# Second feed-forward stage: rows normalised on ScalarE as scale and bias, the residual sum in two halves

## The chip, the cores and the metric

The kernel runs on one core of a Trainium2 chip. A core has TensorE (PE, with its weight loads shown apart as PEld), VectorE (DVE), ScalarE (ACT), GpSimd (POOL) and a queue for transfers (SP), each with its own stream of instructions; they meet at semaphores. The metric is the device time of one execution in microseconds (us); the median of the runs is compared.

## The reference

One transformer block on x of shape 2 x 4096 x 256, in float32:

```python
x = x + 0.5 * ffn(layernorm(x), Wr, We)          # first feed-forward stage
x = x + attention(layernorm(x), ...)             # 16 heads of 16
x = x + 0.5 * ffn(layernorm(x), Wr, We)          # second feed-forward stage

def layernorm(x, eps=1e-05):
    m = mean(x); v = var(x)                      # over the 256 of a row
    return (x - m) / sqrt(v + eps)

def ffn(x, Wr, We):                              # E = 8 experts, TOP_K = 2
    logits = einsum('btd,ed->bte', x, Wr)
    top_vals, top_idx = top_k(logits, 2)
    w = softmax(top_vals)
    # a token is dropped by an expert that is full (C = T*2/8*1.5 + 1)
    return einsum('btk,btkd->btd', w, expert_outputs)
```

## The kernel before

The program has three phases one after the other: the first feed-forward stage with the projections for q, k and v (names beginning with fr_), attention (at_), and the second feed-forward stage with attention's output projection in front of it (bk_). The change is in the third, `back_phase`.

The 8192 rows are worked in 16 groups of 512 rows, each as TG = 4 tiles of 128 rows by 256. The text counts bodies 0 to 15: in body g the experts of group g are computed and, between them, the groups g+1 and g+2 are prepared. Bodies 0 and 1 and the last four stand written out in the program, the ten between are a loop of two bodies a pass. The order on every engine is the order in which the code is written; there is no planner.

The experts. All eight experts are applied to all rows and weighted afterwards, most weights being zero. A body has 16 chunks, numbered 0 to 15 here: four tiles (i) by four pairs of experts (k). A chunk is six matmuls of 128x512 into one of three PSUM banks (`pe_s`, `NB = 3`, `experts`, L1417). VectorE then takes the chunk up with two operations, one for each expert (`combine`, L1547): out = bank * weight + what was summed so far. A bank is used again every third chunk (only the last chunk takes bank 1 early), so TensorE waits at chunk n for VectorE's second operation on chunk n-3.

The preparation of a later group, in the order of its data:

- `spread_out` (PE, L1368) spreads the softmax reciprocals into bank `py[0]`; `normalise_heads` (DVE, L1495) multiplies attention's output by them into `an`; `project` (PE, L1374) multiplies `an` by Wo into both banks `py[0]` and `py[1]`.
- `biased` (POOL, L1637) adds the output bias to the residual x into `xb`; `add_residual` (DVE, L1502) adds `py` and `xb` into `y[u]`, two operations of 128x512.
- `statistics` (DVE, L1510 to L1517) finds mean and variance of the four tiles (`mv`, `var`); `take_root` (ACT, L1459) takes the root; the Newton steps in `normal` (DVE, L1523 to L1527) make one over the root (`rs`), each waiting for the one before.
- the last four operations of `normal` (DVE, L1531) write xn = (y - mean) * rs, one of 128x256 for each tile.
- `turn` (PE, L1384) transposes `xn` into `pT`; `turned` (ACT, L1466 and L1468) copies that to `xt` and `xh`; `lower` (POOL, L1642) makes the low part `xl`; `router` (PE, L1393) makes the logits; `pick` (DVE, L1562 to L1572), `route` (POOL), `exponential` (ACT, L1474), `odds` (DVE), `positions` (PE), `room` (DVE, L1579) and `weigh` (POOL, L1674) make the weights.

In body g, VectorE's turn is: chunks 0 and 1, statistics(g+1), chunks 2 and 3, normal(g+1), chunks 4 and 5, normalise_heads(g+2), chunks 6 to 9, pick(g+1), chunks 10 to 13, odds(g+1), chunks 14 and 15, room(g+1), add_residual(g+2). In body 0 the inversion of the softmax sums of the second batch (`invert_sums`, L1217 to L1221) stands behind pick. TensorE's turn is: chunks 0 to 3, spread_out(g+2), chunks 4 to 7, turn(g+1), chunks 8 and 9, router(g+1), project(g+2), chunks 10 to 15, positions(g+1). ScalarE's is: take_root, turned, exponential.

The first feed-forward stage (`front_phase`) already has the form that the change brings to the third phase: `newton` ends with `nb` = -mean * rs (DVE, L580), and `normalise` (ACT, L476) writes xn.

Of the kernel before, what the change touches and what calls it, by code (L numbers as in the profile page):

```python
# [21 lines left out]
ALU = mybir.AluOpType  # L22
# [3 lines left out]
P = 128  # L26
# [7 lines left out]
TG = 4  # L34
# [7 lines left out]
def hold(eng, sem, value, tick):  # L42

    eng.wait_ge(sem, value)
    eng.sem_inc(tick, 1)
# [31 lines left out]
def need(eng, sem, value):  # L77

    if not (isinstance(value, int) and value <= 0):
        eng.wait_ge(sem, value)  # L80
# [1167 lines left out]
def back_phase(nc, name, shared, ahead, sources, attended_out, out):  # L1248
# [7 lines left out]
    BANK = [n % NB for n in range(CHUNKS - 1)] + [1]  # L1256
    PICKS = 11
    ROUTE = 7
    with ExitStack() as ctx:
        def sb(n, shape, dt=F32):  # L1260
            return ctx.enter_context(nc.sbuf_tensor(f"{name}_{n}", shape, dt))
# [14 lines left out]
        xn, xt = sb("xn", [P, TG, D]), sb("xt", [P, NC, GT])  # L1276
        xh, xl = ([sb(f"{n}{u}", [P, NC, GT], F32R) for u in range(2)] for n in ("xh", "xl"))
        stats, mv = sb("stats", [P, TG, 6]), sb("mv", [P, TG, 2])
        var, root, r0, r1, rs = (sb(n, [P, TG]) for n in ("var", "root", "r0", "r1", "rs"))
        acc, acb = [sb(f"acc{u}", [P, TG, D]) for u in range(2)], sb("acb", [P, 2, D])  # L1280

        t1, t2, left, a0, a1, mask = (sb(n, [P, TG, E]) for n in ("t1", "t2", "left", "a0", "a1", "mask"))
# [32 lines left out]
        def runs(g, ahead):  # L1315

            return not isinstance(g, int) or g + ahead < NG

        with nc.Block() as block:
# [43 lines left out]
            def _(pe):  # L1363
                def spread_out(n, u, it):

                    pe.wait_ge(s_rec[u], it * DMA + DMA)
                    need(pe, s_y, n)
                    pe.matmul(py[0][:, :], spread[:, :], rec[u][:, :], start=True, stop=True).then_inc(s_pr, 1)  # L1368

                def project(n):  # L1370
                    need(pe, s_an, n + 1)
                    for i in range(TG):
                        for c in range(NC):
                            last = pe.matmul(py[i // 2][:, (i % 2) * D:(i % 2 + 1) * D], an[:, c, i * P:(i + 1) * P],  # L1374
                                             wo[:, c, :], start=(c == 0), stop=(c == NC - 1))
                    last.then_inc(s_py, 1)
# [78 lines left out]
            @block.scalar  # L1455
            def _(ac):
                def take_root(n):
                    need(ac, s_var, n + 1)
                    ac.activation(root[:, :], var[:, :], ACT.Sqrt).then_inc(s_root, 1)  # L1459

                def turned(n, u):

                    need(ac, s_tr, n + 1)
                    need(ac, s_xl, n)
                    for c in range(NC):
                        ac.activation(xt[:, c, :], pT[c][:, :], ACT.Copy)  # L1466
                    for c in range(NC):
                        last = ac.activation(xh[u][:, c, :], pT[c][:, :], ACT.Copy)  # L1468
                    last.then_inc(s_ev, 1)

                def exponential(n):
                    need(ac, s_gap, n + 1)
                    need(ac, s_wt, n)
                    ac.activation(ex[:, :], gap[:, :], ACT.Exp).then_inc(s_ex, 1)  # L1474

                take_root(0)
                turned(0, 0)
                exponential(0)

                def body(g, u, it):  # L1480
                    if runs(g, 1):
                        take_root(g + 1)
                        turned(g + 1, 1 - u)
                        exponential(g + 1)

                iterations(ac, body)

            @block.vector
            def _(ve):
# [5 lines left out]
                        last = ve.tensor_tensor(an[:, c, :], at[u][:, c, :], py[0][:, :], ALU.mult)  # L1495
                    last.then_inc(s_an, 1)

                def add_residual(n, u):
                    ve.wait_ge(s_py, n + 1)
                    ve.wait_ge(s_xb, n + 1)  # L1500
                    for k in range(2):
                        last = ve.tensor_tensor(y[u][:, 2 * k:2 * k + 2, :].rearrange("p i d -> p (i d)"), py[k][:, :],  # L1502
                                                xb[:, 2 * k:2 * k + 2, :].rearrange("p i d -> p (i d)"), ALU.add)
                    last.then_inc(s_y, 1)

                def statistics(n, src):

                    hold(ve, s_y, n + 1, s_tick)
                    for i in range(TG):
                        last = ve.bn_stats(stats[:, i, :], src[:, i, :])  # L1510
                    last.then_inc(s_a, 1)
                    hold(ve, s_a, n * 2 + 1, s_tick)
                    for i in range(TG):
                        last = ve.bn_aggr(mv[:, i, :], stats[:, i, :])  # L1514
                    last.then_inc(s_a, 1)
                    ve.wait_ge(s_a, n * 2 + 2)
                    ve.tensor_scalar(var[:, :], mv[:, :, 1], EPS, None, ALU.add).then_inc(s_var, 1)  # L1517

                def normal(n, src):

                    ve.wait_ge(s_root, n + 1)
                    ch = Chain(ve, s_nw, 5, n)
                    ch.step(ve.reciprocal(r0[:, :], root[:, :]))  # L1523
                    ch.step(ve.tensor_tensor(r1[:, :], r0[:, :], r0[:, :], ALU.mult))  # L1524
                    ch.step(ve.tensor_tensor(rs[:, :], r1[:, :], var[:, :], ALU.mult))  # L1525
                    ch.step(ve.tensor_scalar(r1[:, :], rs[:, :], -0.5, 1.5, ALU.mult, ALU.add))  # L1526
                    ch.step(ve.tensor_tensor(rs[:, :], r0[:, :], r1[:, :], ALU.mult))  # L1527
                    ch.close()
                    need(ve, s_tr, n)
                    for i in range(TG):  # L1530
                        last = ve.tensor_scalar(xn[:, i, :], src[:, i, :], mv[:, i, 0:1], rs[:, i:i + 1],  # L1531
                                                ALU.subtract, ALU.mult)
                    last.then_inc(s_xn, 1)

                def combine(g, u, it, i, first=0, end=E):
                    if i == 0 and first == 0:
# [53 lines left out]
                ve.wait_ge(s_bv, 1)  # L1590
                ve.tensor_tensor(bo_sb[:, :], bo_sb[:, :], py[1][:, 0:D], ALU.add).then_inc(s_bo, 1)
                normalise_heads(0, 0, 0)
                add_residual(0, 0)
                statistics(0, y[0])
                normal(0, y[0])
                normalise_heads(1, 1, 0)
                pick(0)
                odds(0)
                room(0)
                add_residual(1, 1)  # L1600

                def body(g, u, it):
                    combine(g, u, it, 0, 0, E // 2)
# [1 line left out]
                        statistics(g + 1, y[1 - u])  # L1605
                    combine(g, u, it, 0, E // 2, E)
                    if runs(g, 1):
                        normal(g + 1, y[1 - u])
                    combine(g, u, it, 1, 0, E // 2)
                    if runs(g, 2):  # L1610
                        normalise_heads(g + 2, u, it + 1)
# [1 line left out]
                    combine(g, u, it, 2, 0, E // 2)  # L1613
                    if runs(g, 1):
                        pick(g + 1)
                    if isinstance(g, int) and g == 0:
                        invert_sums(ve, ahead, 1)
                    combine(g, u, it, 2, E // 2, E)
# [4 lines left out]
                    if runs(g, 1):  # L1623
                        room(g + 1)
                    if runs(g, 2):
                        add_residual(g + 2, u)

                iterations(ve, body)

# [1 line left out]
            def _(gp):  # L1631
                def biased(n, u, it):
                    hold(gp, s_x[u], it * DMA + DMA, s_tick)
                    if not (isinstance(n, int) and n == 0):
                        hold(gp, s_y, n, s_tick)
                    for i in range(TG):
                        last = gp.tensor_tensor(xb[:, i, :], xg[u][:, i, :], bo_sb[:, :], ALU.add)  # L1637
                    last.then_inc(s_xb, 1)
# [150 lines left out]
```

## Time and profile before

| | us |
|---|---|
| median of 3 runs | 6290.88 |
| lowest and highest | 6289.6, 6301.9 |
| the profiled execution | 6298.43 |
| its span | 6296.6 |
| its third phase, from about 5779 to the end | 517 |

| engine | busy us | share of the span |
|---|---|---|
| PE | 6199.1 | 98% |
| DVE | 5929.1 | 94% |
| ACT | 4830.8 | 77% |
| POOL | 398.3 | 6% |

Most of the span is attention, which the change leaves alone. The shares of the whole span therefore tell little of the third phase; its own stretches are read instead. Stretches of the trace are given in us from the start of the span. A row of the timeline has the start, the time, the engine, the line, the operation, what it writes and reads, and how many were merged into the row; in brackets stands the engine's idle time before it and what ended that. A "<-" after an engine in a list of waits names whom it waited for.

### The profile page before, as it was taken

What the parts mean: (1) busy time and instruction counts of PE and PEld (TensorE: products, weight loads), DVE (VectorE), ACT (ScalarE), POOL (GpSimd) and SP (SyncE); (2) the same over time, 40 slices, a digit from 0 to 9 for tenths busy, and PEclk for the clock granted to TensorE, in tenths of its full rate; (3) what the DMA queues carried; (4) which work ended last, traced back from release to release, by engine and by line L of the source; (5) the groups of instructions that cost most, each with busy time, mean ns of one, the idle gap of its engine ahead of it and who ended that gap; (6) DMA issues with size and microseconds to landing.
All of it is one profiled execution on the core that took longest, in us unless ns stands there. A gap on an engine that the chain in (4) does not pass through costs nothing. (4 is left out here: it accounts for less than half of the span.)

```text
span 6296.6 us, 158218 instructions
## 1 busy us (share of the span) xinstructions
PE 6199.1 (98%) x54276; PEld 2765.3 (44%) x54276; DVE 5929.1 (94%) x6835; ACT 4830.8 (77%) x8889; POOL 398.3 (6%) x604
## 2 busy tenths in 40 slices
PE   8998999999999999999999999999999999999999
PEld 6886333333333333333333333333333333334777
DVE  7998999999999999999999999999999999992877
ACT  4443488888888888888888888888888888886111
POOL 3443100000000000000000000000000000000221
PEclk9998699999999999999999999999999999999999
DMA  2334110101010101010101010101010101000110
GB/s 85 121 126 124 25 17 14 17 14 17 13 17 14 17 14 17 14 17 14 17 14 17 14 17 14 17 14 17 14 17 14 17 14 17 3 22 26 60 52 28
DMA packets 121411, 175.90 MB, mean 28 GB/s; under 512 B 62016, under 2 KB 78944, under 8 KB 117728
## 3 DMA queue, kind: packets, MB, share of 16 engines
q1 hardware_dynamic: 120928, 168.25, 11.8%
q8 instruction: 451, 7.39, 0.5%
q14 instruction: 32, 0.26, 0.0%
HBM read 98.47 MB, written 69.73 MB: 27 GB/s over the span
## 5 line engine op out<-in xcount | busy, mean ns | idle before, releaser
L1136 DVE TENSOR_REDUCE at_mx<-at_m 128x1 f32<-128x1024 f32 x4027 | 4927.9, 1224 | 47.6 <-PE at_m L1012 28.1
L1111 ACT ACTIVATE at_ex<-at_s 128x512 f32<-128x512 f32 x8192 | 4450.2, 595 | 612.9 <-PE at_s L1033 44.7
L1033 PE MATMUL at_s<-at_q,at_k 50*128 50x512 f32 x8192 | 2998.4, 444 | 0.0
L1012 PE MATMUL at_m<-at_k,at_q 48*128 48x512 f32 x8032 | 2927.1, 444 | 0.0
L1043 PE MATMUL at_po<-at_ex,at_v 128*32 128x256 f32 x32816 | 2625.8, 392 | 0.0
L1012 PEld LDWEIGHTS at_m<-at_k,at_q 48*128 48x128 f32 x8032 | 1184.3, 185 | 1658.7 <-DVE at_mx L1136 1590.5
L1043 PEld LDWEIGHTS at_po<-at_ex,at_v 128*32 128x32 f32 x32816 | 646.6, 108 | 1489.4 <-issue 749.9
L1033 PEld LDWEIGHTS at_s<-at_q,at_k 50*128 50x128 f32 x8192 | 1212.4, 185 | 42.6 <-ACT at_ex L1111 42.2
L987 POOL COPY at_v<-at_vst 128x1024 f32<-128x1024 f32 x16 | 16.7, 1041 | 4463.6 <-DMA at_vst<-v_by_head 4463.4
L1417 PE MATMUL bk_ps<-sh_weh,bk_xl 128*128 128x512 f32 x512 | 170.1, 413 | 20.2 <-DVE bk_acc L1547 20.1
L1459 ACT ACTIVATE bk_root<-bk_var 128x4 f32<-128x4 f32 x16 | 3.3, 205 | 218.0 <-DVE bk_var L1517 218.0
L1417 PE MATMUL bk_ps<-sh_weh,bk_xh 128*128 128x512 f32 x512 | 160.8, 395 | 0.0
L1417 PE MATMUL bk_ps<-sh_wel,bk_xh 128*128 128x512 f32 x512 | 160.8, 395 | 0.0
L1547 DVE SCALAR_TENSOR_TENSOR bk_acb<-bk_ps,bk_weight,bk_acc 128x256 f32<-128x256 f32 x192 | 92.9, 484 | 71.1 <-PE bk_ps L1417 65.5
L1547 DVE SCALAR_TENSOR_TENSOR bk_acc<-bk_ps,bk_weight,bk_acb 128x256 f32<-128x256 f32 x256 | 123.9, 484 | 9.1
L372 PE MATMUL fr_ps<-sh_weh,fr_xl 128*128 128x512 f32 x352 | 115.5, 409 | 14.4 <-DVE fr_acc L597 14.1
L509 ACT ACTIVATE fr_parts<-fr_rot 128x1024 fp32r<-128x1024 f32 x32 | 34.2, 1069 | 106.0 <-DVE fr_rot L652 106.0
L1417 PEld LDWEIGHTS bk_ps<-sh_weh,bk_xl 128*128 128x128 f32 x512 | 89.5, 188 | 51.2 <-DVE bk_acc L1547 32.7
L372 PE MATMUL fr_ps<-sh_weh,fr_xh 128*128 128x512 f32 x352 | 111.5, 398 | 0.0
L372 PE MATMUL fr_ps<-sh_wel,fr_xh 128*128 128x512 f32 x352 | 111.3, 397 | 0.0
L1466 ACT ACTIVATE bk_xt<-bk_pT 128x512 f32<-128x512 f32 x32 | 17.4, 595 | 119.6 <-PE bk_pT L1384 119.6
L1417 PEld LDWEIGHTS bk_ps<-sh_weh,bk_xh 128*128 128x128 f32 x512 | 96.1, 188 | 23.3
(194 smaller groups left out, 2989.9 us busy)
## 6 DMA issues: line engine op xcount, KB each, us to landing
at_q<-q_parts SPq DMA_DIRECT2D x96, 256.0 KB, 5.0
at_k<-k_parts SPq DMA_DIRECT2D x96, 256.0 KB, 6.3
q_parts<-fr_parts SPq DMA_DIRECT2D x64, 256.0 KB, 2.2
k_parts<-fr_parts SPq DMA_DIRECT2D x64, 256.0 KB, 2.4
attended<-at_o SPq DMA_DIRECT2D x256, 34.0 KB
fr_x<-in_x SPq DMA_DIRECT2D x16, 512.0 KB, 4.3
after_ffn<-fr_acc SPq DMA_DIRECT2D x16, 512.0 KB, 3.0
v_by_head<-fr_v SPq DMA_DIRECT2D x16, 512.0 KB, 4.4
```

What stands on the lines that cost most here:

```text
L372: last = pe.matmul(pe_s[BANK[n]][:, :], (xh, xl)[a][0][u][:, c, i * P:(i + 1) * P], (weh, wel)[b][:, c, EP * k:EP * (k + 1), :].rearrange( ...
L509: ac.activation(pt[:, 0, w, :, :], rot[:, :, :], ACT.Copy).then_inc(s_hi, 1)
L987: gp.tensor_copy(V[p][:, :, :, 0:HD], vst[p][:, :, :, :]).then_inc(s_vh, 1)
L1012: ins = pe.matmul(pm[w][:, h * QB:(h + 1) * QB], Q[p][rows, base + i * P:base + (i + 1) * P], K[p][rows, c * CW + h * QB:c * CW + (h + 1) ...
L1033: pe.matmul(ps[event(t) % NS], K[p][rows, j * P:(j + 1) * P], Q[p][rows, sb_ * QU + g * QB:sb_ * QU + (g + 1) * QB], start=True, stop=True ...
L1043: last = pe.matmul(po[W * t:W * (t + 1), cols], V[p][:, w, j, :], Ex[QUAD * (j % NX) + t][:, cols], start=start and half == 0, stop=stop a ...
L1111: ac.activation(Ex[QUAD * (j % NX) + 2 * g + 1 - half][:, :], ps[event(t) % NS], ACT.Exp)\
L1136: ve.tensor_reduce(out=mx[u][:, i, c:c + 1], in_=first[(RED + k) % len(first)][:, 0:CW] if opens else pm[w][:, :], op=ALU.max, axis=AX.X)\
L1417: last = pe.matmul(pe_s[BANK[n]][:, :], (xh, xl)[a][u][:, c, i * P:(i + 1) * P], (weh, wel)[b][:, c, EP * k:EP * (k + 1), :].rearrange("p ...
L1459: ac.activation(root[:, :], var[:, :], ACT.Sqrt).then_inc(s_root, 1)
L1466: ac.activation(xt[:, c, :], pT[c][:, :], ACT.Copy)
L1547: ve.scalar_tensor_tensor(out=dst, in0=pe_s[BANK[i * NP + e // EP]][:, (e % EP) * D:(e % EP + 1) * D], scalar=weight[u][:, i, e:e + 1], in ...
```

## The change

`normal` is cut in two. VectorE keeps the five Newton steps, now called `newton`, and gets a sixth small operation that writes nb = -mean * rs. ScalarE's new `normalise` waits for it and writes xn = rs * y + nb with four activations of 128x256 (Identity, with scale and bias of each row as operands). It stands between take_root and turned. VectorE now waits for the previous group's xn before it starts the Newton steps.

`add_residual` is cut in two halves, each with its own signal. Half 0 (from `py[0]`) moves to a place behind pick in the middle of chunks 8 to 11, in body 0 ahead of `invert_sums`; half 1 stays at the end of the body. TensorE's waits follow: spread_out waits for half 0 of the group before, and project gets a wait for half 1. At the start of the phase both halves still stand together.

```diff
@@ tensor
                 def spread_out(n, u, it):
                     pe.wait_ge(s_rec[u], it * DMA + DMA)
-                    need(pe, s_y, n)
+                    need(pe, s_y, n * 2 - 1)
                 def project(n):
                     need(pe, s_an, n + 1)
+                    need(pe, s_y, n * 2)
@@ scalar
+                def normalise(n, src):
+
+                    need(ac, s_nw, (n + 1) * NEWTON)
+                    need(ac, s_tr, n)
+                    for i in range(TG):
+                        last = ac.activation(xn[:, i, :], src[:, i, :], ACT.Identity, bias=nb[:, i:i + 1], scale=rs[:, i:i + 1])
+                    last.then_inc(s_xn, 1)
...
                         take_root(g + 1)
+                        normalise(g + 1, y[1 - u])
                         turned(g + 1, 1 - u)
@@ vector
-                def add_residual(n, u):
-                    ve.wait_ge(s_py, n + 1)
-                    ve.wait_ge(s_xb, n + 1)
-                    for k in range(2):
-                        last = ve.tensor_tensor(y[u][:, 2 * k:2 * k + 2, :].rearrange("p i d -> p (i d)"), py[k][:, :],
-                                                xb[:, 2 * k:2 * k + 2, :].rearrange("p i d -> p (i d)"), ALU.add)
-                    last.then_inc(s_y, 1)
+                def add_residual(n, u, k):
+                    if k == 0:
+                        ve.wait_ge(s_py, n + 1)
+                        ve.wait_ge(s_xb, n + 1)
+                    ve.tensor_tensor(y[u][:, 2 * k:2 * k + 2, :].rearrange("p i d -> p (i d)"), py[k][:, :],
+                                     xb[:, 2 * k:2 * k + 2, :].rearrange("p i d -> p (i d)"), ALU.add).then_inc(s_y, 1)
...
-                def normal(n, src):
+                def newton(n):
 
                     ve.wait_ge(s_root, n + 1)
-                    ch = Chain(ve, s_nw, 5, n)
+                    need(ve, s_xn, n)
+                    ch = Chain(ve, s_nw, NEWTON, n)
...
+                    ch.add(ve.scalar_tensor_tensor(out=nb[:, :], in0=mv[:, :, 0], scalar=-1.0, in1=rs[:, :],
+                                                   op0=ALU.mult, op1=ALU.mult))
                     ch.close()
-                    need(ve, s_tr, n)
-                    for i in range(TG):
-                        last = ve.tensor_scalar(xn[:, i, :], src[:, i, :], mv[:, i, 0:1], rs[:, i:i + 1],
-                                                ALU.subtract, ALU.mult)
-                    last.then_inc(s_xn, 1)
...
                     if runs(g, 1):
                         pick(g + 1)
+                    if runs(g, 2):
+                        add_residual(g + 2, u, 0)
                     if isinstance(g, int) and g == 0:
                         invert_sums(ve, ahead, 1)
...
                     if runs(g, 2):
-                        add_residual(g + 2, u)
+                        add_residual(g + 2, u, 1)
```

On VectorE, behind chunk 3 of body 0, the Newton steps ended before with the four operations on xn ahead of chunk 4's first:

```order
L1526 TENSOR_SCALAR bk_r<-bk_rs 128x4 [waits bk_newton]
L1527 TENSOR_TENSOR bk_rs<-bk_r 128x4 [waits bk_newton]
L1531 TENSOR_SCALAR bk_xn<-bk_y,bk_mv,bk_rs 128x256 [waits bk_tr,bk_newton]
L1531 TENSOR_SCALAR bk_xn<-bk_y,bk_mv,bk_rs 128x256 x3
L1547 SCALAR_TENSOR_TENSOR bk_acb<-bk_ps,bk_weight,bk_y 128x256 [waits bk_mm]
```

At the same place on VectorE now:

```order
L1538 TENSOR_SCALAR bk_r<-bk_rs 128x4 [waits bk_newton]
L1539 TENSOR_TENSOR bk_rs<-bk_r 128x4 [waits bk_newton]
L1540 SCALAR_TENSOR_TENSOR bk_nb<-bk_mv,bk_rs 128x4 [waits bk_newton]
L1556 SCALAR_TENSOR_TENSOR bk_acb<-bk_ps,bk_weight,bk_y 128x256 [waits bk_mm]
L1556 SCALAR_TENSOR_TENSOR bk_acc<-bk_ps,bk_weight,bk_acb 128x256 [waits bk_acc]
```

Four operations of 128x256 have left VectorE there, and one of 128x4 has come.

On ScalarE, the same group before, from the root to the exponential's table:

```order
L1459 ACTIVATE bk_root<-bk_var 128x4 [waits bk_var]
L1466 ACTIVATE bk_xt<-bk_pT 128x512 [waits bk_xlow,bk_tr]
L1466 ACTIVATE bk_xt<-bk_pT 128x512
L1468 ACTIVATE bk_xh<-bk_pT 128x512 x2
L1474 ACT_TABLE_LOAD [waits bk_weight]
```

And ScalarE now:

```order
L1461 ACTIVATE bk_root<-bk_var 128x4 [waits bk_var]
L1468 ACTIVATE bk_xn<-bk_y,bk_nb,bk_rs 128x256 [waits bk_tr,bk_newton]
L1468 ACTIVATE bk_xn<-bk_y,bk_nb,bk_rs 128x256 x3
L1476 ACTIVATE bk_xt<-bk_pT 128x512 [waits bk_xlow,bk_tr]
L1476 ACTIVATE bk_xt<-bk_pT 128x512
L1478 ACTIVATE bk_xh<-bk_pT 128x512 x2
L1484 ACT_TABLE_LOAD [waits bk_weight]
```

The four activations stand between root and copies, and no table load has come with them.

On VectorE, the end of pick in body 0 and what follows it, before:

```order
L1566 TENSOR_REDUCE bk_rank<-bk_t 128x4 [waits bk_pick]
L1572 TENSOR_TENSOR bk_sel<-bk_t,bk_rank 128x32 [waits bk_pick]
L1217 RECIPROCAL bk_recs<-bk_sums 128x512 [waits bk_pick,bk_sums]
L1219 CAST bk_split<-bk_recs 128x512 [waits bk_recs]
L1221 TENSOR_TENSOR bk_split<-bk_recs,bk_split 128x512 [waits bk_recs]
L1547 SCALAR_TENSOR_TENSOR bk_acb<-bk_ps,bk_weight,bk_acc 128x256 [waits bk_acc,bk_mm]
```

And now:

```order
L1575 TENSOR_REDUCE bk_rank<-bk_t 128x4 [waits bk_pick]
L1581 TENSOR_TENSOR bk_sel<-bk_t,bk_rank 128x32 [waits bk_pick]
L1514 TENSOR_TENSOR bk_y<-bk_py,bk_xb 128x512 [waits bk_pick,bk_xb,bk_proj]
L1217 RECIPROCAL bk_recs<-bk_sums 128x512 [waits bk_sums]
L1219 CAST bk_split<-bk_recs 128x512 [waits bk_recs]
L1221 TENSOR_TENSOR bk_split<-bk_recs,bk_split 128x512 [waits bk_recs]
L1556 SCALAR_TENSOR_TENSOR bk_acb<-bk_ps,bk_weight,bk_acc 128x256 [waits bk_acc,bk_mm]
```

Half 0 of the residual sum, with its wait for the projection (bk_proj), has come in behind pick; in the other bodies the three rows of L1217 to L1221 are not there.

## Rows read from the trace of the kernel before

**Rows 1.** Windows, body 5: length; busy PE, PEld, DVE, ACT, POOL; clock; DMA.

```profile
5962.37:5993.13 30.76, 29.59 (x142) 23.52 (x142) 23.93 (x68) 5.04 (x8) 7.71 (x18) 1.00 0.17 53
```

**Rows 2.** Waits, 5808 to 6293, engine PE: us in total, times, longest.

```profile
PE bk_ps L1417 <- DVE bk_acc L1547: 20.1, 19, 1.3
```

**Rows 3.** Timeline, TensorE and its weight loads, body 5, chunks 6 and 7.

```profile
5971.47 0.63 PE L1417 MATMUL bk_ps<-sh_weh,bk_xl 128*128 128x512 f32 x2
...
5974.20 0.73 PE L1417 MATMUL bk_ps<-sh_weh,bk_xl 128*128 128x512 f32 x2 [1.17 <-DVE bk_acc L1547]
...
5974.78 0.63 PE L1417 MATMUL bk_ps<-sh_wel,bk_xh 128*128 128x512 f32 x2
...
5975.24 0.62 PE L1417 MATMUL bk_ps<-sh_weh,bk_xh 128*128 128x512 f32 x2
5975.48 1.02 PEld L1384 LDWEIGHTS bk_pT<-sh_ident,bk_xn 128*128 128x128 f32 x8
```

**Rows 4.** Timeline, VectorE, body 5, residual sum to chunk 4; TensorE at chunk 2.

```profile
5963.60 1.28 DVE L1502 TENSOR_TENSOR bk_y<-bk_py,bk_xb 128x512 f32<-128x512 f32 x2
...
5965.25 0.63 PE L1417 MATMUL bk_ps<-sh_weh,bk_xl 128*128 128x512 f32 x2
...
5966.35 0.48 DVE L1547 SCALAR_TENSOR_TENSOR bk_acc<-bk_ps,bk_weight,bk_acb 128x256 f32<-128x256 f32 x1
...
5971.85 1.38 DVE L1531 TENSOR_SCALAR bk_xn<-bk_y,bk_mv,bk_rs 128x256 f32<-128x256 f32 x4
...
5973.15 0.48 DVE L1547 SCALAR_TENSOR_TENSOR bk_acb<-bk_ps,bk_weight,bk_y 128x256 f32<-128x256 f32 x1
5973.67 0.48 DVE L1547 SCALAR_TENSOR_TENSOR bk_acc<-bk_ps,bk_weight,bk_acb 128x256 f32<-128x256 f32 x1
```

**Rows 5.** Timeline, body 5, chunks 13 and 14 start; VectorE takes up chunk 13.

```profile
5988.81 0.63 PE L1417 MATMUL bk_ps<-sh_weh,bk_xl 128*128 128x512 f32 x2
...
5990.21 0.63 PE L1417 MATMUL bk_ps<-sh_weh,bk_xl 128*128 128x512 f32 x2
...
5990.50 0.48 DVE L1547 SCALAR_TENSOR_TENSOR bk_acb<-bk_ps,bk_weight,bk_acc 128x256 f32<-128x256 f32 x1 [0.48 <-PE bk_ps L1417]
```

**Rows 6.** Timeline, first phase, in its loop: nb, VectorE's next operation, ScalarE's xn.

```profile
308.14 0.16 DVE L580 SCALAR_TENSOR_TENSOR fr_nb<-fr_mv,fr_rs 128x4 f32<-128x4 f32 x1
308.34 0.48 DVE L597 SCALAR_TENSOR_TENSOR fr_acb<-fr_ps2z,fr_weight,fr_acc 128x256 f32<-128x256 f32 x1
308.42 2.08 ACT L476 ACTIVATE fr_xn<-fr_acc,fr_nb,fr_rs 128x256 f32<-128x256 f32 x4 [3.70 <-DVE fr_nb L580]
```

**Rows 7.** Timeline, first phase, first group: nb, xn, and the turn waiting for it.

```profile
9.10 0.16 DVE L580 SCALAR_TENSOR_TENSOR fr_nb<-fr_mv,fr_rs 128x4 f32<-128x4 f32 x1
...
9.30 2.07 ACT L476 ACTIVATE fr_xn<-fr_x,fr_nb,fr_rs 128x256 f32<-128x256 f32 x4 [1.23 <-DVE fr_nb L580]
...
11.49 1.14 PEld L338 LDWEIGHTS fr_pT<-sh_ident,fr_xn 128*128 128x128 f32 x6 [11.49 <-issue]
```

**Rows 8.** Timeline, body 5: chunk 10 behind the projection, VectorE's idle time behind pick.

```profile
5984.43 0.81 PE L1417 MATMUL bk_ps<-sh_weh,bk_xl 128*128 128x512 f32 x2
...
5986.31 0.48 DVE L1547 SCALAR_TENSOR_TENSOR bk_acb<-bk_ps,bk_weight,bk_acc 128x256 f32<-128x256 f32 x1 [2.62 <-PE bk_ps L1417]
```

**Rows 9.** Timeline, before body 0: xn of group 0 and its turn.

```profile
5793.34 1.38 DVE L1531 TENSOR_SCALAR bk_xn<-bk_y,bk_mv,bk_rs 128x256 f32<-128x256 f32 x4
5794.77 1.57 PEld L1384 LDWEIGHTS bk_pT<-sh_ident,bk_xn 128*128 128x128 f32 x8 [6.76 <-DVE bk_xn L1531]
```

**Rows 10.** Timeline, body 0: chunk 7, the inversion of sums, chunk 10.

```profile
5819.53 0.73 PE L1417 MATMUL bk_ps<-sh_weh,bk_xl 128*128 128x512 f32 x2 [0.76 <-DVE bk_acc L1547]
...
5829.28 3.35 DVE L1217 RECIPROCAL bk_recs<-bk_sums 128x512 f32<-128x512 f32 x1 [0.16 <-DVE bk_sel L1572]
...
5829.75 0.81 PE L1417 MATMUL bk_ps<-sh_weh,bk_xl 128*128 128x512 f32 x2
```

**Rows 11.** Timeline, VectorE, body 13, chunk 1.

```profile
6214.56 0.48 DVE L1547 SCALAR_TENSOR_TENSOR bk_acb<-bk_ps,bk_weight,bk_acc 128x256 f32<-128x256 f32 x1 [2.73 <-PE bk_ps L1417]
```

More of the change, by code:

```diff
@@ L1258, in back_phase @@
     ROUTE = 7
+    NEWTON = 6
     with ExitStack() as ctx:
@@ L1278, in back_phase @@
         stats, mv = sb("stats", [P, TG, 6]), sb("mv", [P, TG, 2])
-        var, root, r0, r1, rs = (sb(n, [P, TG]) for n in ("var", "root", "r0", "r1", "rs"))
+        var, root, r0, r1, rs, nb = (sb(n, [P, TG]) for n in ("var", "root", "r0", "r1", "rs", "nb"))
         acc, acb = [sb(f"acc{u}", [P, TG, D]) for u in range(2)], sb("acb", [P, 2, D])
@@ L1476, in _ @@
                 take_root(0)
+                normalise(0, y[0])
                 turned(0, 0)
@@ L1496, in normalise_heads @@
                     last.then_inc(s_an, 1)
-                def add_residual(n, u):
-                    ve.wait_ge(s_py, n + 1)
-                    ve.wait_ge(s_xb, n + 1)
-                    for k in range(2):
-                        last = ve.tensor_tensor(y[u][:, 2 * k:2 * k + 2, :].rearrange("p i d -> p (i d)"), py[k][:, :],
-                                                xb[:, 2 * k:2 * k + 2, :].rearrange("p i d -> p (i d)"), ALU.add)
-                    last.then_inc(s_y, 1)
+                def add_residual(n, u, k):
[4 more added lines that the diff above has]
+                                     xb[:, 2 * k:2 * k + 2, :].rearrange("p i d -> p (i d)"), ALU.add).then_inc(s_y, 1)
                 def statistics(n, src):
-                    hold(ve, s_y, n + 1, s_tick)
+                    hold(ve, s_y, n * 2 + 2, s_tick)
                     for i in range(TG):
@@ L1592, in _ @@
                 normalise_heads(0, 0, 0)
-                add_residual(0, 0)
+                for k in range(2):
+                    add_residual(0, 0, k)
                 statistics(0, y[0])
-                normal(0, y[0])
+                newton(0)
                 normalise_heads(1, 1, 0)
@@ L1599, in _ @@
                 room(0)
-                add_residual(1, 1)
+                for k in range(2):
+                    add_residual(1, 1, k)
                 def body(g, u, it):
@@ L1607, in body @@
                     if runs(g, 1):
-                        normal(g + 1, y[1 - u])
+                        newton(g + 1)
                     combine(g, u, it, 1, 0, E // 2)
@@ L1634, in biased @@
                     if not (isinstance(n, int) and n == 0):
-                        hold(gp, s_y, n, s_tick)
+                        hold(gp, s_y, n * 2, s_tick)
                     for i in range(TG):
```

## Prediction

> **What bounds the kernel now.** I read first the busy time of the engines in one body of the third phase, since shares of the whole span say nothing of it. A body takes 30.76 us, TensorE is busy for 29.59 of it, VectorE for 23.93, ScalarE for 5.04, and TensorE's granted clock is 1.00 [rows 1]. So TensorE sets the pace, and only its stalls can be won. The list of waits shows one kind: in bodies 0 to 15 TensorE waits 19 times for VectorE's second operation on a chunk, 20.1 us together, never over 1.3 [rows 2]. One such wait stands in each of bodies 0 to 14 at chunk 7; the other four are in bodies 0, 13 (two) and 14.
>
> The timeline of body 5 shows why. Chunk 7 uses chunk 4's bank again. VectorE does chunk 4 at 5973.15 and 5973.67, so it is done at 5974.15, and chunk 7 starts at 5974.20 [rows 3, 4]. Undisturbed chunks start 1.40 apart [rows 5]; chunk 6 started at 5971.47, so chunk 7 was due at 5972.87. It is 1.33 late, of which the row counts 1.17 as idle. The first pair of matmuls behind a stop takes 0.58 to the next pair (5974.20 to 5974.78) where others take 0.47, another 0.11 [rows 3]. A stall at chunk 7 thus costs **1.44 us**. VectorE is late there because, in the stretch from the end of one body to chunk 4, it has the residual sum, statistics, Newton steps and xn beside the chunks.
>
> **The change part by part.**
>
> xn leaves VectorE. Before, xn starts at 5971.85 and chunk 4 at 5973.15, 1.30 later [rows 4]. Now nb stands in xn's place, and the operation behind an nb starts 0.20 after it [rows 6]. VectorE reaches chunk 4 1.10 us earlier.
>
> Half a residual sum leaves the same stretch. The two halves take 1.28 [rows 4], one 0.64. Not all of it counts: VectorE now comes early enough to wait for chunk 1. A chunk can be taken up 0.29 after the next has started (5990.21, 5990.50) [rows 5]; chunk 2 starts at 5965.25, so chunk 1 can be taken up at 5965.54, and its second operation, 0.52 behind the first (5973.15 to 5973.67), starts at 5966.06 where it started at 5966.35 [rows 4]. This half brings 0.29.
>
> Together: chunk 4 starts on VectorE at 5973.15 - 1.10 - 0.29 = 5971.76 and is done at 5972.76, and chunk 7 may start 0.05 later, at 5972.81. It is due at 5972.87. The stall goes, with 0.06 to spare.
>
> What is late next is xn itself. The turn's weight load begins 0.24 after the last pair of chunk 7 [rows 3]; with chunk 7 at 5972.87 the last pair is at 5973.80 and the turn is due at 5974.04. nb starts at 5971.85 - 0.29 = 5971.56. In the first phase's loop ScalarE starts xn 0.28 after nb's start and needs 2.08 [rows 6]; in its first group, where the turn waits for it, the load comes 0.12 after xn's end (9.30 + 2.07 to 11.49) [rows 7]. That gives 5971.56 + 2.48 = 5974.04: no margin and no loss. ScalarE, idle for most of the body, hides the 2.08 us, but only just. The bounds of the unknown are 0.09 less (the first group's 2.39 from nb to load [rows 7]) and, above, a few tenths. I allow **0.07 a body**.
>
> ScalarE needs no other table: the order shows the same two table loads a body as before.
>
> Half 0 at its new place. Behind pick VectorE is idle for 2.62 until 5986.31 [rows 8]. The projection is over when chunk 10 starts (5984.43), so its signal is there by 5984.43 + 0.29 = 5984.72, half 0 ends at 5985.36, 0.9 before chunk 10 is ready. Cost nothing; if that cover were gone it would be the 0.64. Queued behind this wait are VectorE's chunks 10 and on, for which TensorE waits from chunk 13, but the same projection stands ahead of chunk 10 on TensorE. The wait that project gets is for half 1 of the group before, done most of a body earlier; GpSimd's bias sum starts 0.64 earlier and has half a body of slack. I cost all three at nothing.
>
> The start of the phase. There the turn waits for xn with nothing to cover it. Before: 5793.34 to 5794.77, 1.43 [rows 9]. Now 2.39 from nb's start [rows 7]. All of the start stands behind it: **+0.96**.
>
> Body 0. Half 0 stands ahead of the inversion of sums, which started at 5829.28 [rows 10]. It must now wait for the projection: 5829.75 + 0.29 = 5830.04, + 0.64, + 0.12 for the sums' own wait = 5830.80. The inversion, and the chunks behind it, for which TensorE already waits there, move by **+1.5**.
>
> Bodies 13 and 14. VectorE stands still for 2.73 at chunk 1 of body 13, although chunk 1 was long ready [rows 11]; it is behind in all of that body and again in body 14. Its whole saving counts, 1.10 + 0.64, about 1.7 in each.
>
> Body 0's stall at chunk 7 is 0.76 instead of 1.17 [rows 10], so it costs 1.03.
>
> **The sum.** Bodies 1 to 12: 12 x 1.44 = 17.3. Body 0: 1.0. Bodies 13 and 14: 3.4. Together 21.7; as a check, all recorded waits with their restarts are 20.1 + 19 x 0.11 = 22.2 [rows 2]. Against it 0.96 + 1.5 + 15 x 0.07 = 3.5. The gain is **18.2 us**. The profiled execution took 6298.43, so it would take 6280.2; the median of the runs shown is 7.6 lower, and the same gain from 6290.88 gives **6272.7**.
>
> **The rivals.**
>
> *The turn becomes the wait.* The two margins above are 0.06 and 0.00 us, and every 0.1 us by which xn comes late costs 1.5 us in 15 bodies. If ScalarE's step is 0.5 us longer than in the first phase (it reads y while VectorE works in the same memory, and waits for two semaphores in the loop), the gain is 21.7 - 2.5 - 7.5 = 11.7, and the time **6279**. For it: xn costs VectorE 1.38 and ScalarE 2.08 for the same four tiles [rows 4, 6]. Against it: the 128 activations of the first phase ran under the same company. The Trainium skill ("ScalarE: Activation LUTs", Rules for kernel authors) says to put additions and multiplications on VectorE, not on ScalarE. The trace agrees that ScalarE is the slower at it; by that rule alone this rival would be the case, by the rows it costs only what sticks out behind chunk 7.
>
> *Half 0 holds up VectorE.* If the projection's signal came later than 0.9 us after my 5984.72, each further 1 us would cost some 14 us in 14 bodies; at 1.5 us late the time would be 6272.7 + 14 x 0.6 = **6281**. No row speaks for it.
>
> *A bigger gain.* The 2.73 stop of body 13 is no wait for data; with other instructions around it, it may fall where VectorE has slack: up to 2.7 more, and with no lag at the turn 1 more: **6269**.
>
> *Slower.* The same stop, met in the loop. It looks like a stop of VectorE's own stream, and the change alters what stands in the loop (fewer large operations, more small ones and waits). Were it to come once in each of the ten bodies of the loop, it would cost 27.3 against the 18.2: **6300**. It decides from 1.8 us a body. Against it: no body of the loop before shows one, and the loop is hardly longer.
>
> **How the numbers follow.** The forecast, 6270 to 6277: 0.62. The bigger gain: 0.10. The turn as the wait: 0.17. Half 0 holding up VectorE: 0.05. Slower: 0.04; 0.02 is left for a median that falls among the higher runs, since those before go from 6289.6 to 6301.9. About 0.2% is what a measurement of this kernel can tell from no change, here 12.6 us, a bound at 6278.3. Faster takes the forecast, the bigger gain and a little of the turn's case: 0.74. Within 0.2%: 0.21. Slower: 0.05. The range must hold 8 in 10: from 6266 (the bigger gain, and the runs' own spread) to 6283 (the turn's case).
>
> **What would show it.** In a body of the loop: a length of 29.3 to 29.4 instead of 30.76; no wait of TensorE at chunk 7; ScalarE's four xn in 2.08 from about 0.3 after nb; the turn's load within 0.1 of where chunk 7 lets it be. If the turn's row names ScalarE's xn with some tenths of idle time, the first rival holds. Behind pick a 0.68 operation on y, ended before chunk 10's first. Before body 0 the turn 0.96 later, in body 0 the inversion 1.5 later against pick and TensorE waiting longer at chunk 13. I am wrong if a body stays above 30 us, or if attention's length differs by more than a few us between the two, for which nothing in the change gives a reason.

## The result and the profile after

The changed kernel takes **6273.55 us** in the median of seven runs (6271.92 to 6286.21), the kernel before 6290.88 (6289.60 to 6301.90, seven runs). The ratio is 0.9973 with a 95% interval of 0.9964 to 0.9982: 17.3 us faster, outside the 0.2% that the prediction takes as no change. The forecast was 6272.7, inside 6266 to 6283.

The profiled execution of after took 6273.55, its span is 6271.7. That is 24.9 less than the profiled execution of before. Only part of it is the change. The third phase begins with the bias matmul of L1426 at 5770.56, and at 5779.17 before: 8.6 us lie in phases whose code is the same. Over eight more kernels with that same code it begins between 5770.1 and 5781.4. From that matmul to the end of the span are 517.4 us before and 501.1 now, a gain of **16.3**, where the sum on record said 18.2. This length is what the kernels are compared by below.

A body of the loop, from one positions matmul to the next, as in [rows 1] (length; busy PE, PEld, DVE, ACT, POOL; clock):

```profile
5952.26:5981.56 29.30, 29.30 (x141) 23.64 (x140) 22.89 (x65) 7.13 (x12) 7.72 (x18) 1.00 0.17 56
```

TensorE is busy all of it. Its waits for VectorE in the list of waits (us in total, times, longest), as in [rows 2]:

```profile
PE bk_ps L1419 <- DVE bk_acc L1556: 5.6, 3, 3.7
```

Nineteen waits have become three, one of them in body 0 and two in body 13. The timeline of body 5, VectorE and ScalarE at chunk 4, then TensorE at chunk 7 and the turn, answers [rows 3, 4]:

```profile
5961.51 0.16 DVE L1540 SCALAR_TENSOR_TENSOR bk_nb<-bk_mv,bk_rs 128x4 f32<-128x4 f32 x1
5961.60 0.48 DVE L1556 SCALAR_TENSOR_TENSOR bk_acb<-bk_ps,bk_weight,bk_y 128x256 f32<-128x256 f32 x1
5961.70 2.09 ACT L1468 ACTIVATE bk_xn<-bk_y,bk_nb,bk_rs 128x256 f32<-128x256 f32 x4 [2.93 <-DVE bk_nb L1540]
...
5962.80 0.62 PE L1419 MATMUL bk_ps<-sh_weh,bk_xl 128*128 128x512 f32 x2
...
5963.73 0.63 PE L1419 MATMUL bk_ps<-sh_weh,bk_xh 128*128 128x512 f32 x2
5963.96 1.02 PEld L1386 LDWEIGHTS bk_pT<-sh_ident,bk_xn 128*128 128x128 f32 x8
```

nb has taken xn's place on VectorE. Chunk 7's row has no brackets: it starts 0.47 behind the pair before it, like any other. The turn's load starts 0.23 behind chunk 7's last pair (5963.73 to 5963.96; 0.24 in [rows 3]), and 0.17 behind the end of xn (5961.70 + 2.09 = 5963.79).

Half 0 behind pick, in the same body, answers [rows 8]:

```profile
5972.92 0.81 PE L1419 MATMUL bk_ps<-sh_weh,bk_xl 128*128 128x512 f32 x2
...
5973.31 0.69 DVE L1514 TENSOR_TENSOR bk_y<-bk_py,bk_xb 128x512 f32<-128x512 f32 x1 [1.13 <-PE bk_py L1376]
5974.79 0.49 DVE L1556 SCALAR_TENSOR_TENSOR bk_acb<-bk_ps,bk_weight,bk_acc 128x256 f32<-128x256 f32 x1 [0.79 <-PE bk_ps L1419]
```

It comes 0.39 behind chunk 10's first matmul, ends at 5974.00, and VectorE then still waits 0.79 for chunk 10. It is free.

The loop is as forecast. Body 0 is not. It took 31.38 before and takes 34.82. VectorE and TensorE there, as in [rows 10]:

```profile
5815.18 0.48 DVE L1556 SCALAR_TENSOR_TENSOR bk_acc<-bk_ps,bk_weight,bk_acb 128x256 f32<-128x256 f32 x1
5819.51 0.48 DVE L1556 SCALAR_TENSOR_TENSOR bk_acb<-bk_ps,bk_weight,bk_acc 128x256 f32<-128x256 f32 x1 [3.85 <-issue]
...
5823.07 0.69 DVE L1514 TENSOR_TENSOR bk_y<-bk_py,bk_xb 128x512 f32<-128x512 f32 x1 [0.23 <-DVE bk_sel L1581]
5823.68 3.34 DVE L1217 RECIPROCAL bk_recs<-bk_sums 128x512 f32<-128x512 f32 x1
...
5829.18 0.95 PE L1419 MATMUL bk_ps<-sh_weh,bk_xl 128*128 128x512 f32 x2 [3.74 <-DVE bk_acc L1556]
5829.93 1.06 PE L1419 MATMUL bk_ps<-sh_wel,bk_xh 128*128 128x512 f32 x2
5830.78 1.06 PE L1419 MATMUL bk_ps<-sh_weh,bk_xh 128*128 128x512 f32 x2
```

Between chunks 8 and 9 VectorE stands for 3.85 us and waits for nothing that the profile shows ("issue"). Pick, half 0, the inversion and chunk 10 follow without a gap and are all late, and TensorE stands for 3.74 at chunk 13. When it starts again, its pairs of matmuls come 0.85 apart and not 0.47. Chunk 9 is ready for nearly all of the 3.85: TensorE is past its last matmuls at 5815.85. The windows of that place (same columns as above) show why the pairs are slow:

```profile
5824.90:5829.10 4.20, 0.54 (x3) 0.11 (x1) 4.10 (x5) 0.00 (x0) 0.30 (x2) 1.00 0.00 0
5829.10:5833.00 3.90, 3.82 (x10) 3.03 (x11) 2.93 (x9) 0.00 (x0) 0.00 (x0) 0.56 0.00 0
5833.00:5837.00 4.00, 4.00 (x20) 3.10 (x19) 2.88 (x8) 0.00 (x0) 1.15 (x5) 1.00 0.01 4
```

TensorE's granted clock is 0.56 in the stretch behind the wait, that is mostly 1.2 GHz and not 2.4. In windows of 1 us over body 0 the clock missing comes to **1.71 us** (1 less the clock, times the length), and to none in body 0 of before. The Trainium skill ("TensorE: Matmul & The Clock Gate", Part 1) says that an idle TensorE is put back to half its clock and that work releases it; this trace agrees, with 0.56 behind 3.74 us of standing still.

### The profile page after: what moved, and what is told of

Read it like the earlier page. It is cut to its first block and busy times, and to the rows that moved or that the text cites. A ratio compares the mean times of both kernels' runs of the same rounds, so it can differ in the third digit from the quotient of the medians.

```text
span 6271.7 us, 158274 instructions
## 1 busy us (share of the span) xinstructions
PE 6186.4 (99%) x54276; PEld 2764.7 (44%) x54276; DVE 5911.4 (94%) x6787; ACT 4862.4 (78%) x8953; POOL 398.5 (6%) x604
## 5 line engine op out<-in xcount | busy, mean ns | idle before, releaser
L1419 PEld LDWEIGHTS bk_ps<-sh_wel,bk_xh 128*128 128x128 f32 x512 | 96.7, 189 | 23.1
```

Source lines behind the costliest of these rows:

```text
L1419: last = pe.matmul(pe_s[BANK[n]][:, :], (xh, xl)[a][u][:, c, i * P:(i + 1) * P], (weh, wel)[b][:, c, EP * k:EP * (k + 1), :].rearrange("p ...
```

## The experiments

Every experiment starts from the changed kernel. The phase is counted from the bias matmul to the end of the span, a loop body is the mean of bodies 2 to 11.

Where an experiment has one run, its single time stands in the last column, and only the lengths are used.

| kernel | phase | body 0 | loop body | body 13 | median or single time |
|---|---|---|---|---|---|
| before | 517.4 | 31.38 | 30.76 | 33.30 | 6290.88 |
| after | 501.1 | 34.82 | 29.31 | 31.69 | 6273.55 |
| xn_alone | 505.6 | 34.22 | 29.58 | 33.22 | 6281.84 |
| split_alone | 514.7 | 32.85 | 30.47 | 32.70 | 6289.70 |
| half_behind_sums | 500.6 | 34.68 | 29.31 | 31.70 | 6283.81 |
| xn_one_more | 503.9 | 34.46 | 29.53 | 31.92 | 6278.62 |
| xn_three_more | 520.1 | 34.73 | 30.52 | 33.01 | 6296.32 |
| pad_twelve | 499.6 | 34.34 | 29.31 | 30.53 | 6273.49 |
| sums_early | 496.1 | 29.29 | 29.31 | 31.99 | 6268.33 (6 runs) |
| sums_early_pad | 495.1 | 29.29 | 29.31 | 30.58 | 6271.87 (7 runs) |

**Each half of the change alone.** xn_alone puts both halves of the residual sum back to the end of the body:

```
                     if runs(g, 1):
                         pick(g + 1)
-                    if runs(g, 2):
-                        add_residual(g + 2, u, 0)
...
                     if runs(g, 2):
-                        add_residual(g + 2, u, 1)
+                        for k in range(2):
+                            add_residual(g + 2, u, k)
```

> The changed kernel with the residual sum whole again at the end of the body: only xn has gone to ScalarE. Theory (the two parts do different shares of the work): VectorE gains 1.10 us of the 1.44 us stall, it finishes chunk 4 at 0.18 behind chunk 7's due time, so a stall of 0.2 to 0.35 us stays at chunk 7 and a body of the loop takes 29.6 to 29.7 us. Rival (moving xn alone is enough, the split brings nothing): 29.3 us a body and no wait at chunk 7.

A loop body took 29.58, within 0.02 of the lower end of the theory's 29.6 to 29.7. xn is worth 1.18 of the 1.45 us that a body gains, and half 0's place 0.27. Body 13 of this kernel, 33.22 long and so 1.53 longer than after's, is worth a look too. VectorE's stop makes TensorE wait there once, for 1.92 (in after twice, for 1.56 and 0.33), and the clock falls behind it, which it does not do in body 13 of after:

```profile
6204.35 0.73 PE L1419 MATMUL bk_ps<-sh_weh,bk_xl 128*128 128x512 f32 x2 [1.92 <-DVE bk_acc L1556]
...
6205.30:6209.30 4.00, 3.98 (x13) 2.58 (x12) 3.79 (x9) 2.07 (x4) 0.00 (x0) 0.57 0.02 4
```

A clock of 0.57 over 4.00 us is 1.72 us missing.

split_alone keeps the halves where the change has them and gives xn back to VectorE:

```
-                        normalise(g + 1, y[1 - u])
                         turned(g + 1, 1 - u)
...
-                    ch.add(ve.scalar_tensor_tensor(out=nb[:, :], in0=mv[:, :, 0], ...))
                     ch.close()
+                    need(ve, s_tr, n)
+                    for i in range(TG):
+                        last = ve.tensor_scalar(xn[:, i, :], src[:, i, :], mv[:, i, 0:1], rs[:, i:i + 1],
+                                                ALU.subtract, ALU.mult)
+                    last.then_inc(s_xn, 1)
```

> The changed kernel with xn back on VectorE: only the residual sum is in two halves. Theory: VectorE would gain 0.64 us but must wait for chunk 1, so 0.29 us comes through, and a body of the loop takes 30.47 us, with a wait of about 0.9 at chunk 7. Rival (a microsecond taken from VectorE's stretch always comes through): 0.64 us, 30.12 us a body.

The loop body was 30.47 with 0.90 of waiting at chunk 7, as the theory had it: 0.29 less than before. So the 0.29 of the prediction comes through as it said; beside the 1.18 of xn_alone the two make 1.47, for 1.45 measured together. Body 0 of this kernel is the clean test of the 1.5 there, since VectorE has no long stop in it:

```profile
5824.53 0.69 DVE L1512 TENSOR_TENSOR bk_y<-bk_py,bk_xb 128x512 f32<-128x512 f32 x1 [1.13 <-PE bk_py L1376]
5825.14 3.34 DVE L1217 RECIPROCAL bk_recs<-bk_sums 128x512 f32<-128x512 f32 x1
...
5830.64 0.73 PE L1419 MATMUL bk_ps<-sh_weh,bk_xl 128*128 128x512 f32 x2 [1.96 <-DVE bk_acc L1556]
5831.21 0.63 PE L1419 MATMUL bk_ps<-sh_wel,bk_xh 128*128 128x512 f32 x2
```

Half 0 waits for the projection, the inversion for half 0, and TensorE waits 1.96 at chunk 13 where it waited 0.50 before: +1.46, and the body is 1.47 longer. Behind this wait the pairs stay 0.57 and 0.47 apart, and no clock is missing.

**Body 0: half 0's place or VectorE's stop.** half_behind_sums moves half 0 behind the inversion in body 0:

```
-                    if runs(g, 2):
-                        add_residual(g + 2, u, 0)
                     if isinstance(g, int) and g == 0:
                         invert_sums(ve, ahead, 1)
+                    if runs(g, 2):
+                        add_residual(g + 2, u, 0)
```

> The changed kernel with half 0 of the residual sum behind the inversion of the sums in body 0 instead of ahead of it; nothing else differs. Body 0 took 34.82 us, 3.4 more than before the change. Theory A (VectorE's stop of 3.85 us at chunk 9 makes the loss, half 0 only its 0.7 us): the stop stays, the wait at chunk 13 falls from 3.74 to about 3.0 us, body 0 takes about 34 us. Theory B (half 0 ahead of the inversion makes the loss, as my prediction had it): body 0 falls to about 31 us or less.

Body 0 was 34.68, the wait at chunk 13 3.61 and VectorE's stop 3.78. So the stop, and not half 0's place, makes this body long; a body of 31 or less is ruled out. I had expected 34 and a wait of 3.0: half 0 no longer delays the inversion, but it still stands ahead of chunk 10, so its 0.6 is paid all the same. xn_alone, which has no half 0 there, gives that 0.6 back (3.15 of waiting).

sums_early moves the inversion to the start of the phase, where VectorE is idle for most of the time:

```
                 normalise_heads(1, 1, 0)
+                invert_sums(ve, ahead, 1)
                 pick(0)
...
-                    if isinstance(g, int) and g == 0:
-                        invert_sums(ve, ahead, 1)
```

> The changed kernel with the inversion of the second batch's sums taken out of body 0 and put ahead of the first pick, where VectorE is idle for 3.67 us at the start of the phase. Theory: in body 0 the stop, the inversion and half 0 only hurt because they stand in one row ahead of chunk 10; without the inversion VectorE has chunk 10 done in time, there is no wait at chunk 13, TensorE's clock does not fall behind it, and body 0 takes 29.3 to 29.6 us; the start grows by 0.8 to 1.2 us (4.5 us of inversion against 3.67 idle). Together 4.0 to 4.7 us less than the changed kernel, near 6269 us. Rival (the stop costs its time wherever it falls): body 0 stays above 32 us and the time at 6272 to 6275 us.

Body 0 is 29.29, and TensorE waits nowhere in it, although VectorE still stops, for 2.67 ahead of chunk 8:

```profile
5817.27 0.48 DVE L1556 SCALAR_TENSOR_TENSOR bk_acb<-bk_ps,bk_weight,bk_y 128x256 f32<-128x256 f32 x1 [2.67 <-issue]
...
PE bk_ps L1419 <- DVE bk_acc L1556: 2.2, 2, 1.8
```

Without the 4.45 us of the inversion behind pick (5823.68 to 5828.13 in after), the three banks and the projection cover a stop of 2.67. The start of the phase got 0.30 longer, for 0.8 to 1.2 expected; three kernels whose code is the same up to body 0 (after, xn_alone, half_behind_sums) have 29.65, 29.71 and 29.27 there, so 0.30 can't be told from none. The phase is 5.0 shorter than after's, and the medians differ by 5.2; the ratio to before is 0.9967 (0.9954 to 0.9979), whose interval overlaps after's, so it is the lengths in the profiled execution and not the ratios that separate the two.

**What VectorE's stop is.** In body 13 of all ten traces, and in body 0 of nine, a transfer of instructions (8 KB) starts on queue 14 between 1.7 and 2.0 us ahead of the end of VectorE's stop; in body 0 of sums_early_pad one starts 1.8 ahead of the end of an idle time of 0.61 that the profile puts down to TensorE. A second transfer follows each 2.4 to 4.0 us later, and no stop goes with it. The share of queue 14 in the stretch 5817.6 to 5818.2 of after (packets, MB, share of 16 engines) shows the one that belongs to 5819.51:

```profile
q14 instruction: 1, 0.01, 3.2%
```

From 5815.8 to 5817.6, the first half of the stop, the queue has none. If the stop is VectorE fetching its own code, it belongs to a place in the instruction stream. pad_twelve puts twelve writes of zeros (128x4, overwritten later) ahead of body 0:

```
                 normalise_heads(1, 1, 0)
+                for j in range(12):
+                    ve.memset(acb[:, 0, 4 * j:4 * j + 4], 0.0)
                 pick(0)
```

> The changed kernel with twelve small memsets of 128x4 on VectorE ahead of the first pick, where it is idle for 3.67 us; no other instruction moves. It tests what VectorE's stop in body 0 is. Theory (it waits for its own code, which comes in pieces of a fixed size): the stop sits at a fixed place of the instruction stream, so it now falls about twelve operations earlier in body 0, at chunk 4 instead of chunk 9, and lasts 2 us or more. Rival (it waits for data of TensorE's or for a transfer of rows): the stop stays at chunk 9.

```profile
5815.07 1.28 DVE L1507 TENSOR_TENSOR bk_an<-bk_at,bk_py 128x512 f32<-128x512 f32 x2 [1.88 <-issue]
...
5824.27 0.69 DVE L1514 TENSOR_TENSOR bk_y<-bk_py,bk_xb 128x512 f32<-128x512 f32 x1 [1.13 <-PE bk_py L1376]
5824.88 3.34 DVE L1217 RECIPROCAL bk_recs<-bk_sums 128x512 f32<-128x512 f32 x1
...
5830.38 0.73 PE L1419 MATMUL bk_ps<-sh_weh,bk_xl 128*128 128x512 f32 x2 [1.95 <-DVE bk_acc L1556]
5830.95 0.77 PE L1419 MATMUL bk_ps<-sh_wel,bk_xh 128*128 128x512 f32 x2
5831.51 1.05 PE L1419 MATMUL bk_ps<-sh_weh,bk_xh 128*128 128x512 f32 x2
```

The stop has moved from ahead of chunk 9 to ahead of normalise_heads, eight large operations earlier, and is 1.88 long. I had expected it at chunk 4, two chunks earlier still, and 2 us or more. The transfer on queue 14 has moved with it: it starts 17.5 us behind the positions matmul in after and 11.3 behind it here. In body 13 the stop moved and shrank too (2.71 ahead of chunk 3 in after, 1.35 in the middle of the statistics here), and that body from 31.69 to 30.53. In body 0 half 0 now waits for the projection, and TensorE waits 1.95 at chunk 13, as the prediction's working had it (2.0). But the body is still 34.34, because TensorE waits 1.06 more at chunk 9 and its clock falls a little later (pairs 0.86 apart from 5831.51 on). The clock missing is 1.71 again. It is 1.71 in body 0 of all six kernels in which it falls, with waits at chunk 13 of 2.60 to 3.74 or, here, of 1.06 and 1.95 within 13 us, and 0.00 in split_alone, with 0.79 and 1.96.

sums_early_pad has both edits:

```
                 normalise_heads(1, 1, 0)
+                for j in range(12):
+                    ve.memset(acb[:, 0, 4 * j:4 * j + 4], 0.0)
+                invert_sums(ve, ahead, 1)
                 pick(0)
```

> This is the version with the inversion of sums ahead of group 1's pick, with twelve small writes of zeros (128x4, overwritten later) ahead of that inversion on VectorE; all else is computed as before. Theory: VectorE's stop of 1.8 to 3.9 us stands at a fixed place of the instruction stream, so twelve more instructions move it to earlier work. In body 0 it leaves chunk 8 (where it cost nothing, since the inversion no longer stands behind pick), so body 0 stays at 29.3. In body 13 the stop shrinks from 2.98 to about 1.3 us, and the body from 31.99 to about 30.5, as the twelve writes did for the changed kernel (31.69 to 30.53). The start of the phase gets 0.15 longer. In all 1.3 us less than the version without the writes: 6267.0, with body 0 at 29.3, the loop's bodies at 29.31 and the phase from the first bias matmul on at 494.8. Rival: the stop goes by time and load, not by place; then body 13 stays at 31.99 and the whole is 6268.5. The two medians are closer than a timing resolves; the lengths of bodies 0 and 13 in the profiled execution decide.

Body 0 stayed at 29.29, with no stop in it that can be told from a wait for TensorE, body 13 went from 31.99 to 30.58, and the phase was 495.1, for 494.8 expected. The stop goes by its place. The median, 6271.87, is above that of sums_early (ratio to before 0.9968, 0.9957 to 0.9979): the 1.0 us of the phase is lost in what the same code ahead of it varies by, and sums_early keeps the lowest median measured, though not a ratio that can be told from this one's (0.9967 and 0.9968).

**How much room the turn has.** xn_one_more and xn_three_more lengthen ScalarE's step by whole activations that write a tile which nobody reads; the output is the same. This is the first; the second has 3 in place of 1.

```
                     need(ac, s_tr, n)
+                    for i in range(1):
+                        ac.activation(spare[:, i, :], src[:, i, :], ACT.Identity, bias=nb[:, i:i + 1], scale=rs[:, i:i + 1])
                     for i in range(TG):
                         last = ac.activation(xn[:, i, :], ...)
```

> The changed kernel with one more activation of 128x256 ahead of the four xn, written to a tile that nobody reads: ScalarE's step is 0.49 us longer. Theory (the turn is covered with almost nothing to spare: xn ends 5963.79, load at 5963.96, about 0.05 of slack): the turn comes 0.44 later, the wait of TensorE there names ScalarE's xn, a body of the loop takes 29.30 + 0.44 = 29.74 us. Rival (TensorE has slack elsewhere in the body that takes it up, or the step is hidden by more than it seems): 29.3 to 29.4 us.

> The same with three more activations, 1.48 us. Theory: 29.30 + 1.43 = 30.73 us a body, so that nearly all of the change's gain is gone, and 15 bodies add 21 us to the changed kernel's 6273.6. Rival (a longer step is partly hidden): clearly under 30.5 us a body.

```profile
PE bk_pT L1387 <- ACT bk_xn L1471: 14.4, 15, 1.0
```

One activation more (0.49) made the loop body 0.22 longer, between the two expectations. Three (1.48) made it 1.21 longer, again between the two, and the list of waits, of xn_three_more here, then names xn in 15 bodies. Both leave the same remainder: 0.49 - 0.22 = 0.27 and 1.48 - 1.21 = 0.27. The turn has **a quarter of a microsecond** of room, and what comes after it is paid in full. Most of the room lies between the weight load, which xn releases, and the first matmul of the turn: the load starts 0.23 ahead of it in after (5963.96 and 5964.19), and together with it where xn is late (5814.89 and 5814.90 in body 0 of xn_one_more).

## Why the prediction was right, and where it was wrong

| part | predicted | measured |
|---|---|---|
| start of the phase | +0.96 | +0.78 (28.87 to 29.65) |
| body 0, with its lag of 0.07 | +0.54 | **+3.44** |
| bodies 1 to 12, with their lag | -16.4 | -17.3 |
| bodies 13 and 14, with their lag | -3.3 | -3.2 (-1.61, -1.56) |
| sum | -18.2 | -16.3 |

**Chunk 7** was right to a few hundredths: 1.44 a body expected, 1.45 measured, no wait left. Predicted from nb's place, VectorE's chunk 4 should be done 0.06 ahead of need. With half 0's part taken out (xn_alone), a body loses 0.27 again, which is what a margin near nothing gives.

**The turn** was sized with a margin of 0.00 and an allowance of 0.07 a body. The allowance wasn't needed (0.9 us in all), the margin is about 0.25. Two of its terms were a little high: ScalarE starts 0.28 behind nb's start in only some bodies (2 and 4) and 0.19 in others (3 and 5), and where the load waits for xn it comes 0.05 behind xn's end and not 0.12. And I had asked when the weight load would be late, where the time is lost only when the matmul behind it is. The rival "the turn becomes the wait" was nearer than its place in the result tells: it needed a step longer by 0.25, and the 0.5 that I gave it would have cost 0.25 a body.

**The start** went as described:

```profile
5784.72 0.16 DVE L1540 SCALAR_TENSOR_TENSOR bk_nb<-bk_mv,bk_rs 128x4 f32<-128x4 f32 x1
5784.92 2.07 ACT L1468 ACTIVATE bk_xn<-bk_y,bk_nb,bk_rs 128x256 f32<-128x256 f32 x4 [1.26 <-DVE bk_nb L1540]
5787.04 1.57 PEld L1386 LDWEIGHTS bk_pT<-sh_ident,bk_xn 128*128 128x128 f32 x8 [7.65 <-ACT bk_xn L1468]
```

From nb to the load are 2.32, not 2.39, against 1.43 before [rows 9]: 0.89 of the 0.96, of which 0.78 reached body 0. The 0.78 is no better known than the 0.44 by which the start varies with the same code (29.27 to 29.71 in after, xn_alone and half_behind_sums).

**Body 0** is the step that failed: "move by +1.5" and the 1.03 gained at chunk 7. Both happen (split_alone for the one, no wait at chunk 7 in after for the other). What is missing is 2.9 us, and it has two parts of like size. VectorE's stop made the wait at chunk 13 3.74 instead of 2.0, and that wait took TensorE's clock down, which cost 1.71. That is 3.45, more than the 2.9. The other side of it is in before: from chunk 13's start to the positions matmul its TensorE took 4.63 (5834.79 to 5839.42), where three undisturbed chunks take 4.20. These 0.43 are small gaps behind the wait that was there already, they are not there any more beside the slow clock, and the prediction had left them out; the 0.07 of lag didn't come either.

I had seen the stop of 2.73 in body 13 [rows 11], had called it a stop of VectorE's own stream, and had let it play for both sides, as a bigger gain and as the slower rival. I had not asked where its like stood in body 0. It was in the trace of before, 1.07 us long and paid by nobody:

```profile
5822.21 0.48 DVE L1547 SCALAR_TENSOR_TENSOR bk_acc<-bk_ps,bk_weight,bk_acb 128x256 f32<-128x256 f32 x1
5823.76 0.48 DVE L1547 SCALAR_TENSOR_TENSOR bk_acb<-bk_ps,bk_weight,bk_acc 128x256 f32<-128x256 f32 x1 [1.07 <-PE bk_ps L1417]
```

The change took four large operations out of every group and put a small one and a wait in, and the place is no longer at chunk 7 but at chunk 9, just ahead of pick, half 0 and the inversion. That the first moved the second is inferred from pad_twelve, where more instructions ahead moved it the other way.

**Bodies 13 and 14** gave 1.61 and 1.56 of the 1.7 each, the stop of body 13 being as long as before, but at chunk 3 and no longer at chunk 1:

```profile
6196.52 0.48 DVE L1556 SCALAR_TENSOR_TENSOR bk_acb<-bk_ps,bk_weight,bk_acc 128x256 f32<-128x256 f32 x1 [2.71 <-PE bk_ps L1419]
```

The forecast of 6272.7 was 0.85 below the median. The misses in the phase come to 1.9 us; the rest is in what the same code ahead of it varies by, and is luck.

## What to carry over

Work taken off the engine that holds up the critical one is worth its time only up to the next limit, so list both margins before believing the sum, and ask of each whether the load or the matmul behind it is what comes late. Long work on the supporting engine (here 4.45 us of inversion) belongs where that engine is idle at the start of a phase: behind pick it had no cover left, and any stop ahead of it went straight to TensorE. A wait of TensorE of 2 us or more can cost more than it shows, since the clock fell behind most of those seen here; price it with the slow matmuls that follow.

## What the runs showed of the hardware

VectorE stops in straight-line code for 0.84 to 3.91 us, with its inputs ready for all or nearly all of that time, at a place that instructions written ahead of it move. The profile puts this down to "issue" or to the last semaphore. The Trainium skill ("Runtime: NRT & Kernel Launch", Instruction fetch mechanics) says that fetching code is mostly hidden, and that a taken branch to code not yet there stalls. If VectorE's stop is the fetch, the trace differs, with 3.85 us in a body that is written out. That it is the fetch is inferred, from two things: the transfer on queue 14 ahead of every such end, and the move of both by twelve small instructions. The profile doesn't name the engine that the queue serves. What sets when the transfer starts, and with it the length, stays open: in body 0 three kernels gave 3.85, 3.78 and 3.91 at chunk 9, others 0.84 to 3.43 (split_alone and xn_one_more the ends), sums_early_pad none that shows.

TensorE's clock cost 1.71 us each time it fell in body 0, whatever the wait, and it fell after 1.06 and 1.95 but not after 0.79 and 1.96. In body 13 of xn_alone it fell after a single wait of 1.92. So the length of the wait alone doesn't decide it; what does was not tried.
